# Products of the identity, into a bank that nothing reads, at the ends of six attentions and beside two gates of a small vision tower

## The reference

```python
h = tokenizer(x, ...)
for block in (L0_attn, L0_ffn, L1_attn, L1_ffn, L2_attn, L2_ffn, L3_attn, L3_ffn):
    h = layernorm(h + block(h, ...))

# L1_ffn, and L3_ffn alike
probs = softmax(xf @ Wg.T + bg)                       # 8 experts
top_w, top_idx = top_k(probs, 2)
combine = zeros((t, 8)).at[arange(t)[:, None], top_idx].add(top_w)
hw = (einsum('td,erd->ter', xf, A) + ba) * combine[:, :, None]
delta = (einsum('ter,eor->to', hw, Bm) + combine @ bb) * SCALING
q, k, v = heads(xf @ Wqkv.T + bqkv + delta)           # 12 heads of 16
attn = softmax(einsum('bhsd,bhtd->bhst', q, k) * SCALE)
out = merge(einsum('bhst,bhtd->bhsd', attn, v)) @ Wproj.T + bproj
```

## Time and profile before

| | us |
|---|---|
| median of 3 executions | 1151.77 (1146.94 to 1162.23) |
| the profiled execution, its own time | 1161.12 |
| its span, first to last instruction | 1159.3 |
| PE busy | 896.2 (77% of the span) |
| PE weight load busy | 761.6 (66%) |
| DVE busy | 528.1 (46%) |
| ACT busy | 332.3 (29%) |
| POOL busy | 261.9 (23%) |
| mean granted TensorE clock | 0.834 of 2.4 GHz |

### The profile page before, as it was taken

How to read it: one execution, slowest core, us unless ns; L and a number is a source line. 1 busy time by engine, 2 the same in 40 slices (tenths; PEclk the granted TensorE clock), 3 DMA queues, 4 the chain that set the end, 5 groups by cost and what they waited for, 6 DMA issues and landing times. The chain is left out here.

```text
span 1159.3 us, 31081 instructions
## 1 busy us (share of the span) xinstructions
PE 896.2 (77%) x13412; PEld 761.6 (66%) x13412; DVE 528.1 (46%) x1168; ACT 332.3 (29%) x677; POOL 261.9 (23%) x289
## 2 busy tenths in 40 slices
PE   8889986998369906899856795777779999387594
PEld 5578863886369905778755673655479999265472
DVE  1469963445343155554423365462821111464464
ACT  0247732212112202442442232333101212133132
POOL 1169840330134323210100101111033322200100
PEclk9989997778579967898876697785969999588598
DMA  7168757400458020000005100000438991100000
GB/s 211 29 142 184 177 154 227 102 1 1 136 168 222 23 63 1 2 3 1 2 1 139 47 4 1 2 3 27 124 83 208 259 222 14 30 3 1 2 4 23
DMA packets 58450, 88.29 MB, mean 76 GB/s; under 512 B 10756, under 2 KB 45000, under 8 KB 58340
## 3 DMA queue, kind: packets, MB, share of 16 engines
q1 hardware_dynamic: 53220, 81.85, 26.7%
q0 software_dynamic: 5120, 4.88, 2.2%
HBM read 78.30 MB, written 7.30 MB: 74 GB/s over the span
## 5 line engine op out<-in xcount | busy, mean ns | idle before, releaser
L2647 DVE TENSOR_TENSOR L_ffnhid<-L_ffnact_gate,L_ffnbank_u 128x300 f32<-128x300 f32 x32 | 15.0, 468 | 118.9 <-ACT L_ffnact_gate L2666 112.4
L1810 POOL TENSOR_SCALAR stage_hat_x<-stage_hat_x 128x320 f32<-128x320 f32 x40 | 51.2, 1280 | 20.4 <-ACT stage_hat_x L1786 20.4
L1720 PE MATMUL ps_places<-stage_own_y,stage_spread 80*64 80x128 f32 x800 | 54.8, 285 | 0.0
L1870 DVE TENSOR_TENSOR stage_product<-ps_rows,stage_hat_x 128x960 f32<-128x960 f32 x40 | 46.3, 1158 | 18.5 <-PE ps_rows L1731 15.2
L1731 PE MATMUL ps_rows<-stage_strip,stage_hat_y 64*32 64x96 f32 x3200 | 49.8, 256 | 6.3 <-DMA stage_strip<-in_strips 3.2
L1731 PEld LDWEIGHTS ps_rows<-stage_strip,stage_hat_y 64*32 64x32 f32 x3200 | 40.6, 108 | 13.4 <-issue 13.4
L1720 PEld LDWEIGHTS ps_places<-stage_own_y,stage_spread 80*64 80x64 f32 x800 | 44.9, 142 | 6.2 <-issue 0.8
L1110 PE MATMUL L_attnbank_q<-L_attnhT,L_attnwq 128*128 128x200 f32 x192 | 42.7, 369 | 6.9 <-DVE L_attnqT L1275 6.7
L2580 POOL DMA_INDIRECT stage_y_rows<-L_ffndown,stage_choice_index x16 | 25.4, 1589 | 90.4 <-ACT L_ffndown L2673 57.0
L1875 DVE TENSOR_REDUCE stage_samples<-stage_product 128x120 f32<-128x960 f32 x40 | 45.7, 1144 | 0.0
L1818 POOL TENSOR_TENSOR stage_hat_x<-stage_rel_x,stage_w_column 128x160 f32<-128x160 f32 x80 | 35.2, 461 | 45.8 <-POOLq L1522 45.8
(11 more groups left out here) (427 smaller groups left out, 2227.5 us busy)
## 6 DMA issues: line engine op xcount, KB each, us to landing
stage_strip<-in_strips SPq DMA_DIRECT2D x80, 189.0 KB, 3.6
L_ffn_win<-in_L_ffn_Win SPq DMA_DIRECT2D x10, 1152.0 KB
stage_L_ffn_win<-in_L_ffn_Win SPq DMA_DIRECT2D x6, 1152.0 KB
L_ffnranks<-stage_ranks SPq DMA_DIRECT2D x16, 400.0 KB
L_ffn_win<-in_L_ffn_Win SPq DMA_DIRECT2D x8, 768.0 KB
L_ffn_wout<-in_L_ffn_Wout SPq DMA_DIRECT2D x10, 576.0 KB
stage_L_ffn_wout<-in_L_ffn_Wout SPq DMA_DIRECT2D x6, 576.0 KB
L_ffn_wout<-in_L_ffn_W SPq DMA_DIRECT2D x8, 384.0 KB
```

The source lines that it names most:

```text
L1720: mm = nc.tensor.matmul(ps_places[HALF_P * h:HALF_P * (h + 1), p % 2, g * P:(g + 1) * P], k.spread[:, p * GRID + g, :], places[:, h * P:(h ...
L1810: nc.gpsimd.tensor_scalar(x, x, 1.0, 1.0, ALU.min, ALU.subtract).then_inc(s["hat_x"], 1)
L1870: nc.vector.tensor_tensor(products(i % 2), in_psum(i % 2), weights_x(i % BUFFERS), ALU.mult).then_inc(s["multiplied"], 1)
```

## The change

A helper `fill` issues products of the identity (the stationary operand) with 512 columns of some weights that lie in SBUF (`idle_rows`) into a PSUM bank. They wait for nothing and nobody waits for them. They are put

- into the last step of every attention: 2 ahead of `turn_out(7)` and 2 ahead of `project_out(7)`; in `branch_attention` the last step but for its first half, so also after `mix_values(7)`;
- behind the last projection of every attention but the last (`last=True` for L3_ffn): 8;
- into `lora_gate`, as the PE stream of that block, in a PSUM bank of its own: 12.

That makes 12 in each of L0_attn, L1_attn, L1_ffn, L2_attn and L3_attn, 4 in L3_ffn, and 12 in each of the two gates: 88. The streams of the other engines are not touched.

```diff
+def fill(tw, bank, moving, times):
+
+    for _ in range(times):
+        tw.nc.tensor.matmul(bank, tw.identity[:], moving, start=True, stop=True)
...
@@ rope_attention
+            idle_rows = w["qk"][:, 0].rearrange("q b z n -> q (b z n)")[:, 0:512]
...
+                if i > TILES:
+                    fill(tw, bank_s[:, 0], idle_rows, 2)
                 if i >= 2:
                     turn_out(i - 2)
...
+                if i > TILES:
+                    fill(tw, bank_s[:, 0], idle_rows, 2)
                 if i >= 2:
                     project_out(i - 2)
+            fill(tw, bank_s[:, 0], idle_rows, 8)
...
@@ attention
+            idle_rows = w["qk"][:].rearrange("q k n -> q (k n)")[:, 0:512]
...
+                if i > TILES:
+                    fill(tw, bank_s[:, 0], idle_rows, 2)
                 if i >= 2:
                     turn_out(i - 2)
...
+                if i > TILES:
+                    fill(tw, bank_s[:, 0], idle_rows, 2)
                 if i >= 2:
                     project_out(i - 2)
+            if not last:
+                fill(tw, bank_s[:, 0], idle_rows, 8)
...
@@ branch_attention
                 if ahead:
                     project_queries(f, 5)
+                else:
+                    fill(tw, bank_s[:, 0], idle_rows, 2)
                 if back:
                     turn_out(s + 1)
                 if f + 1 < PAIRS:
                     turn_tokens(f + 1)
+                if not ahead:
+                    fill(tw, bank_s[:, 0], idle_rows, 2)
                 if back:
                     project_out(s + 1)
+            fill(tw, bank_s[:, 0], idle_rows, 8)
...
@@ lora_gate
-    with nc.Block() as block:
+    with nc.psum_tensor(name + "ps_idle", [P, 512], F32) as ps_idle, nc.Block() as block:
+
+        @block.tensor
+        def _(pe):
+            fill(tw, ps_idle[:], idle_rows, 12)
```

More of the change, by code:

```diff
@@ L522, in _, with attention @@
                 pool.wait_ge(rotated[FIRST_Q], f + 1)
-def attention(tw, name, kind, w, given=None):
+def attention(tw, name, kind, w, given=None, last=False):
     nc = tw.nc
@@ L1167, in project_out @@
                 mm.then_inc(y_in_psum, 1)
+            idle_rows = w["Wo"][:].rearrange("q c k n -> q (c k n)")[:, 0:512]
             turn_tokens(0)
@@ L2132, in pick_two, with lora_gate @@
                                                  in1=x[:, :, 0:8], op0=ALU.mult, op1=ALU.add))
-def lora_gate(tw, m, name, bg):
+def lora_gate(tw, m, name, bg, idle_rows):
     nc = tw.nc
@@ L2934, in stage @@
                 front(tw, m, l, gate[0], 8, fetch=(lambda sp: weights6.load(sp, range(3))) if l == "L1_ffn" else None)
-                lora_gate(tw, m, l, gate[1])
+                lora_gate(tw, m, l, gate[1], w["qk"][:].rearrange("q k n -> q (k n)")[:, 0:512])
                 spread_gate(tw, m, l, extra > 0)
-                attention(tw, l, "adapted", w, given=m)
+                attention(tw, l, "adapted", w, given=m, last=l == "L3_ffn")
             plan[i] = stage
```

## The result

The first four executions of the changed kernel had a median of 1211.32 us (1207.82 to 1214.90), those of the kernel before 1156.95 (1146.94 to 1162.23): a ratio of 1.047 with an interval of 1.0407 to 1.0532. It is slower, by 54 us where 49 were forecast, and 0.3 us above the upper end of the range. The profiled execution is one of 1207.82 us, 46.7 us longer in time and span than the profiled one of before.

The account below looks back on a forecast made before the run. TensorE's lower clock, low at stage joints and in short attentions, was taken as a real cost. Ends +39.9, gates +15.4, turns −2.5 and fronts −3.5 gave +49: 1151.8 + 49 = 1201 us; own range 1192 to 1210, 8-in-10 range 1179 to 1211.

Parts of the forecast that it names:

- a product at the full clock, at half: Each 512-column float32 product on PE counts as two rows: 0.86 us at full clock, 1.71 at half.
- end of L1_ffn, L3_attn: At these ends nothing hides the 12 products; PE drains after ACT and delays the next stage: +7.9 us each.
- end of L2_attn: Clock starts at 0.50 and rises 5 us after the dense work begins, so the products delay this end by +9.4 us.
- gates: In both gates the 12 products take 12.8 us against DVE's 5.1 us chain: +7.7 us each, 15.4 together.
- turns behind the gates: With the clock up, PE's turns of the widened choice behind both gates get shorter: 2.5 us saved.
- fronts, all four: Clock stays up for the first 1.6 to 3.1 us of each `front`: 3.5 us saved in all four.
- Rival B: At stage ends and gates, the drain does not hold the barrier for products in the array: +31 us, 1182; chance 0.14.
- Rival A: Products keep the clock up through each whole `front` and into the first projections: +27 us, 1179; chance 0.10.
- Rival C: A product on PE is one row, 0.43 us, like a transpose: +12 us, 1164, within 2%; chance 0.05.
- the estimate from the Trainium skill: About 131 ns per 512-column matmul, four float32 passes: 0.52 us a product, sum +20, 1172; trace spoke against it.
- the last but one: Whole-kernel step carrying the +49 us sum, unscaled, onto the runs' median: 1151.8 + 49 = 1201, 4.3% slower.
- another phase of the clock: Prediction called wrong if the attentions' untouched loops differ by more than a few us through this; no chance given.

Follow-up runs that it names:

- two later profiles: The changed kernel, unchanged, run and profiled a second and third time: means of 1204.2 and 1210.3 us, profiled executions of 1201.3 and 1204.0 us.
- the loops' products: Kernel before plus 20 products only in PE's waits in the loops of L1_attn (12) and L2_attn (8): 1138.0 us, ratio 0.983; 1139.4 over nine executions.
- 40 at the joints: Kernel before plus 40 products fitted to holes at last projections, gates and attention starts: 1144.5 us, ratio 0.989.

## Why the prediction came out as it did

By its own steps, with the first profile of after and, where they differ from it by more than 0.1 us, the two later ones:

| term | forecast | measured | two later profiles |
|---|---|---|---|
| a product at the full clock, at half | 0.86, 1.71 | 0.855, 1.71 | |
| end of L1_ffn, L3_attn | +7.9 each | +7.8, +7.8 | |
| end of L0_attn | +7.8 | +7.7 | |
| end of L2_attn | +9.4 | +8.7 | |
| end of L1_attn | +4.1 | +4.0 | |
| end of L3_ffn | +2.8 | +2.7 | |
| gates | +15.4 | +8.2, +7.4 | +7.5, +7.5 |
| turns behind the gates | −2.5 | −1.7, −0.9 | |
| fronts, all four | −3.5 | −5.5 | −3.4, −3.3 |
| sum | +49 | +46.3 | +47.9, +47.9 |

L0_attn's end answers to the earlier trace rows (PE free at 287.89, next stage at 301.26), L2_attn's to the earlier trace rows (816.34 and 830.77). That one is shorter than forecast because the clock rose 3.7 us after the products began, not 5. A `front` is taken from the stage's start to DVE's copy of the gate's sums. The measured 46.3 leaves 0.4 of the two profiles' 46.7 us, but that is partly luck: stage by stage the remainders lie between −1.0 and +1.6 us and cancel. Against the later profiles the remainders are −7.7 and −5.0, mostly the 12 us by which L1_attn is shorter in them.

Rival B is out: the drain holds the barrier for products in the array, DVE starts 1.03 us after the last one. Rival A is out for this kernel: the clock fell in all four fronts, in all three profiles. That it can carry over shows in one `front` of one other profile, that with two products behind the last projections. Rival C is out, and with it the estimate from the Trainium skill ("TensorE: Matmul & The Clock Gate", "Back-to-back issue gap"). The trace gives 0.855 us for a product and 7.8 us for the end of L1_ffn. The same section has for a single matmul of 512 columns at the full clock a gap of about 216 ns; four of these, an estimate, are 0.86 us.

**The step that failed** is the last but one: "on the median of the runs, 1151.8 + 49 = 1201". The median of three executions was taken for the level of the kernel, and the profiled execution, 0.8% above it, for an outlier. Over 58 executions the level is 1155.9 (1156.8 with the five highest): 4 us of the miss. Another 4 lie between the sum and the measured difference: 53.0 over all executions, 49 in the prediction, 48.2 with the loops' products in both kernels. The last 2 are between the median of the first four executions, 1211.3, and the changed kernel's mean, 1208.9.

The second 4 have no place in the parts that were changed, which add 46 to 48 us in all three profiles. But these are the shortest executions of their series: their mean is 1204.4 where all fourteen have 1208.9. So the missing time lies in executions without a profile, and no trace here can place it. The profiles show where executions differ: in L1_attn ahead of its tail (178.8, 167.1 and 167.1 us), and in L0_attn ahead of its tail (92.8, 95.2 and 95.1 us, where the profiles of before have 91.5 and 91.6). Up to there the two programs have the same instructions on every engine, and four kernels that differ from the one before only later in the program have 91.5 to 95.4. Whether the mean of these loops moves with the change, or the samples differ, stays open; 3 us is the uncertainty. On the profiled execution itself the sum came close: 1161.1 + 49 = 1210, where 1207.8 was measured. That is partly luck too, for the later profiled executions are at 1201.3 and 1204.0.

The term that the prediction put at nothing is the clock in the loops that the change does not touch. It read the low slices of the earlier trace rows as those of the joints and the short attentions. In fact 25 of the 40 slices are below 9, and those of the loops in L0_attn and L1_attn are among them. A smaller slip changes no sum: in the tail of L1_attn the clock is at 0.50 from 614.6 already, not from 615.2.

**The range** was too narrow for the same reason. "0.7% between executions" was put around 1201 and ended at 1210, though a kernel whose own executions spread from 1146 to 1171 gives a difference of small samples that spreads as well. The prediction named what would make it wrong, "another phase of the clock" in the untouched loops, and gave it no chance. At 12 us in L1_attn alone it was the largest unknown of the case.

## What to carry to other kernels

A product that only keeps TensorE busy is free inside a wait of PE that is longer than itself, and costs its full price where PE is the last engine at a barrier: count the slack first (here 1.8 us behind the last projection held two, and eight ended 5.3 us past ACT). Look also for the waits of 2 to 3 us in a steady loop, not only for the long ones at the joints: they come back with each turn of the loop, and filling them gave 17 us with 20 products, where 40 at the joints gave 11 (the intervals of the two overlap). Before an absolute time is forecast from a few executions, look whether they form one level; where the clock falls by luck, forecast the difference, and widen the range by the falls that could come or go.

## What the runs showed of the hardware

The same wait of PE, 2.44 us for the same instruction of ACT, was followed by 6 us at a granted clock of 0.50 in some executions and by none in others. L1_attn took 184 or 196 us with one and the same program. I had counted the falls at the joints and taken the loops' for fixed. In ten profiles of ten the falls of this loop went with what happened early in the stage: three falls behind a wait of 4.77 us and 6.8 us at 0.50, one behind 3.3 us, none behind 3.1. With the later waits cut to 0.72 us no profile showed a fall there, though all six had the early one. In L2_attn a wait of 2.15 us ahead of a score was followed by 34 us at 0.50, and the same wait at 1.5 us by no fall in five profiles of the six with the loops' products and by one of 17 us in the sixth.

The Trainium skill describes such a loop ("TensorE: Matmul & The Clock Gate", "HAM oscillation — how this bites in real kernels"), in which every turn starts cold behind a wait for a DMA; here the waits are shorter than those it names, and the fall is not certain but a matter of the execution.

The slower executions are those with the lower mean clock: the loops' products alone took 1135.6 us at 0.860 and 1146.7 at 0.844.
